# Four taps in place of three ahead of the vector engine, from the second image on, with new order tables

## The reference, cut to what matters

```python
x = x + conv_block(_ln_c(x))          # per image
#   qkv = conv 1x1 (256 -> 768)
#   agg = conv 1x1 grouped(conv 5x5 depthwise(qkv, padding=2))
#   q, k, v of qkv and of agg; relu on q and k
#   out = q (k^T [v, 1]) ; out[..., :-1] / (out[..., -1:] + 1e-15)
#   proj 1x1 (512 -> 256), batch norm with given mean and variance
t = t + ffn(_ln_t(t))                 # 1024 tokens of 256 per image
#   weights of 6 experts from softmax(mean token @ router), top 2 of 11
#   sum over experts of w_e * (gelu(t W1_e + b1_e) W2_e + b2_e)
```

## Time and profile before

| | us |
|---|---|
| median of 3 runs (1488.21 to 1489.84) | 1489.03 |
| the profiled execution, its own time | 1490.25 |
| its span in the trace | 1488.5 |
| PE busy | 1368.5 (92%) |
| DVE busy | 1255.1 (84%) |
| ACT busy | 1058.4 (71%) |
| POOL busy | 964.1 (65%) |

### The profile page before, as it was taken

How to read it: one execution, slowest core, us unless ns; L and a number is a source line. 1 busy time by engine, 2 the same in 40 slices (tenths; PEclk the granted TensorE clock), 3 DMA queues, 4 the chain that set the end, 5 groups by cost and what they waited for, 6 DMA issues and landing times.

```text
span 1488.5 us, 18705 instructions
## 1 busy us (share of the span) xinstructions
PE 1368.5 (92%) x6844; PEld 779.7 (52%) x6844; DVE 1255.1 (84%) x1281; ACT 1058.4 (71%) x1887; POOL 964.1 (65%) x736
## 2 busy tenths in 40 slices
PE   5996788899999999999999999999999998999997
PEld 3445645555655556555655556555655555544343
DVE  5999499999999999999999999999999996950100
ACT  4454465778678877878687877977787857765775
POOL 5265557567678668756776677856865757445644
PEclk8997799899999999999999999999999999999999
DMA  6010000000002000100001000100000000100000
GB/s 227 31 57 0 0 29 1 0 30 15 0 1 72 15 0 1 43 29 15 1 0 72 15 1 1 43 15 0 1 35 9 15 1 1 43 15 1 15 15 15
DMA packets 14251, 32.75 MB, mean 22 GB/s; under 512 B 2384, under 2 KB 5328, under 8 KB 13904
## 3 DMA queue, kind: packets, MB, share of 16 engines
q1 hardware_dynamic: 14160, 31.56, 6.1%
...
## 4 chain that ended last, share of the span: by engine, by line
PE 63%; DVE 16%; ACT 9%; POOL 6%; issue 5%; DMA 1%; SPq 0%; POOLq 0%; ACTq 0%; DVEq 0%
PE wbk L504 23%; PE acc L517 16%; DVE dacc L1125 13%; PE wbk L621 7%; PE wbk L631 3%; PE wbk L595 3%; PE wbk L580 3%; PE wbk L607 3%; PE wbk L575 2%; POOL gl L968 2%; PE wbk L614 1%; ACT hb L735 1%; ACT hb L832 1%; ACT gh L734 1%; POOL dwo L938 1%
## 5 line engine op out<-in xcount | busy, mean ns | idle before, releaser
L1125 DVE SCALAR_TENSOR_TENSOR dacc<-qkvs,dww,dacc 128x960 f32<-128x960 f32 (+4 forms) x930 | 1026.9, 1189 | 0.0
L968 POOL TENSOR_TENSOR gl<-hb,gh 128x512 f16<-128x512 f32 x256 | 303.8, 1194 | 241.3 <-ACT hb L735 239.8
L938 POOL TENSOR_TENSOR dwo<-dwo,tapb 128x992 f32<-128x992 f32 (+2 forms) x100 | 227.2, 2272 | 118.6 <-ACT tapb L709 88.7
L832 ACT ACTIVATE hb<-wbk,b1s 128x512 f32<-128x512 f32 x256 | 174.5, 684 | 113.5 <-PE wbk L504 105.6
L517 PE MATMUL acc<-gh,w2h 128*128 128x512 f16 x512 | 194.9, 381 | 7.1 <-POOL gl L968 6.2
L517 PE MATMUL acc<-gl,w2h 128*128 128x512 f16 x512 | 194.8, 380 | 0.0
L517 PE MATMUL acc<-gh,w2l 128*128 128x512 f16 x512 | 194.7, 380 | 0.0
L734 ACT ACTIVATE gh<-hb,ewg 128x512 f16<-128x512 f32 x256 | 183.3, 716 | 2.6 <-PE acc L517 1.3
L735 ACT ACTIVATE hb<-hb,ewg 128x512 f32<-128x512 f32 x256 | 182.6, 713 | 0.0
L504 PE MATMUL wbk<-th,w1h 128*128 128x512 f16 x512 | 154.1, 383 | 11.7 <-ACT rb L823 4.6
L504 PE MATMUL wbk<-tl,w1h 128*128 128x512 f16 x512 | 153.7, 382 | 0.0
...
## 6 DMA issues: line engine op xcount, KB each, us to landing
...
```

Of the source, the lines that this page charges most:

```text
L832: last = nc.scalar.activation(hb[:, f % GB, :], b[:], ACT.Gelu, bias=b1s[:, f % FT:f % FT + 1], scale=1.0 / (X_SCALE * W_SCALE))
L938: ins = nc.gpsimd.tensor_tensor(d3[:, oy, ox], d3[:, oy, ox], t3[:, iy, ix], ALU.add)
L968: nc.gpsimd.tensor_tensor(gl[:, f % GB, :], hb[:, f % GB, :], gh[:, f % GB, :], ALU.subtract).then_inc(g_low, 1)
L1125: ins = nc.vector.scalar_tensor_tensor(out=dst[:, oy, ox], in0=i3[:, jy, jx], scalar=dww[:, m, tap:tap + 1], in1=a3[:, oy, ox], op0=ALU.mu ...
```

## The change

Image 1's tiles 2 and 3 (the keys of the second image) have no base taps. All other tiles of images 1 to 7 have four in place of three; the fourth is the tap two rows above the centre. Image 0 is as before. All five tables are written anew, and so are the places of DVE's small tasks.

```diff
     if s == 0:
         return DIAG_BASE if m in DIAG_TILES else []
-    return BASE_TAPS[:3]
+    if s == 1 and m in (2, 3):
+        return []
+    return BASE_TAPS[:4]
```

One line of FIRST and one of END, and the places:

```diff
-squares.0.0.0 squares.0.0.1 sums.0.0 weights.0 weights.2 stats.0.0 rnorm.0.0 means.0 rbc.0.0.0 rbc.0.0.1
+squares.0.0.0 squares.0.0.1 sums.0.0 weights.2 weights.0 stats.0.0 rnorm.0.0 rbc.0.0.0 rbc.0.0.1 means.0
...
-apply.-1.1.0 apply.-1.1.1 high.-1.1.0 high.-1.1.1 low.-1.1.0 low.-1.1.1 S G G logits.-1 F S F S G F exp.-1 S
+apply.-1.1.1 F G high.-1.1.0 S high.-1.1.1 low.-1.1.0 F G low.-1.1.1 S F S F logits.-1 exp.-1 G F S G F G G
...
-AGG_PLACES = {1: (20, 24, 76, 81), 2: (17, 25, 78, 87), 7: (20, 23, 75, 84), 8: (19, 21, 75, 83)}
-RAW_PLACES = {0: (89, 90), 1: (64, 68), 2: (66, 72), 7: (69, 74)}
+AGG_PLACES = {1: (20, 25, 75, 80), 2: (17, 23, 79, 82), 7: (16, 20, 80, 84), 8: (19, 21, 75, 83)}
+RAW_PLACES = {0: (86, 87), 1: (63, 66), 2: (66, 67), 7: (66, 72)}
```

More of the change, by code:

```diff
@@ new lines @@
+matrices.0.1 qkv.0.1.0 qkv.0.1.1 sums.1.0 stats.1.0 rnorm.1.0 b b diag.0.0.0 rbc.1.0.0 rbc.1.0.1 apply.1.0.0
+apply.1.0.1 b diag.0.0.1 b diag.0.1.0 high.1.0.0 tok.0.0 b low.1.0.0 high.1.0.1 diag.0.1.1 tok.0.1 tok.0.2
+tok.0.3 tok.0.4 b tok.0.5 b b tok.0.6 tok.0.7 b relu_q.0.0 b kv.0.0.0 b kv.0.0.1 mask.0.0 relu_q.0.1
+att.0.0.0 att.0.0.1 att.0.0.2 att.0.0.3 scale.0.0.0 att.0.0.4 att.0.0.5 att.0.0.6 att.0.0.7 b b scale.0.0.1
+back.0.0.0.0 back.0.0.0.1 back.0.0.1.0 back.0.0.1.1 agg.0.2.0 low.1.0.1 agg.0.2.1 agg.0.3.0 agg.0.3.1
@@ L179 @@
[L179 to L188, removed]
@@ new lines @@
+b b stats.-1.1 kv.0.0.1 mask.0.0 rnorm.-1.1 b F S relu_q.0.1 att.0.0.0 b S att.0.0.1 att.0.0.2 att.0.0.3
+rbc.-1.1.0 rbc.-1.1.1 G F scale.0.0.0 att.0.0.4 apply.-1.1.0 apply.-1.1.1 att.0.0.5 att.0.0.6 att.0.0.7
+scale.0.0.1 qkv.1.2.1 S S G F high.-1.1.0 high.-1.1.1 low.-1.1.0 low.-1.1.1 logits.-1 qkv.1.3.0 back.0.0.0.0
+back.0.0.0.1 back.0.0.1.0 back.0.0.1.1 qkv.1.3.1 G S agg.0.2.0 agg.0.2.1 F exp.-1 squares.2.0.0 F F F
+squares.2.0.1 sums.2.0 agg.0.3.0 agg.0.3.1 G G G S stats.2.0 G G S rnorm.2.0 F F F S b G S G S b G S
@@ L201 @@
[L201 to L205 removed]
+agg.-1.0.0 S F agg.-1.0.1 agg.-1.1.0 agg.-1.1.1 S G att.-1.1.0 att.-1.1.1 att.-1.1.2 G F qkv.0.0.0 G
@@ new lines @@
+rbc.-1.1.0 rbc.-1.1.1 apply.-1.1.0 G F apply.-1.1.1 scale.0.0.0 att.0.0.4 att.0.0.5 att.0.0.6 G S att.0.0.7
+scale.0.0.1 high.-1.1.0 qkv.1.2.0 qkv.1.2.1 high.-1.1.1 F qkv.1.3.0 b S back.0.0.0.0 low.-1.1.0 low.-1.1.1
+logits.-1 b S qkv.1.3.1 back.0.0.0.1 back.0.0.1.0 back.0.0.1.1 agg.0.2.0 G F agg.0.2.1 agg.0.3.0
+squares.2.0.0 squares.2.0.1 sums.2.0 F exp.-1 agg.0.3.1 S b G G stats.2.0 b F F S G G S rnorm.2.0 F G S F F
+G S b S b F S G F agg.0.4.0 rbc.2.0.0 G rbc.2.0.1 apply.2.0.0 S G F agg.0.4.1 S b apply.2.0.1 agg.0.5.0
@@ L218 @@
-G F F agg.0.4.1 S b b agg.0.5.0 agg.0.5.1 G S S G G S F F G S kv.0.1.0 G F F S G F G S G S F b S G kv.0.1.1
-F F S b G G F mask.0.1 S F b b S b G S
+rnorm.-1.1 G G relu_q.0.1 F att.0.0.0 rbc.-1.1.0 rbc.-1.1.1 apply.-1.1.0 apply.-1.1.1 att.0.0.1 att.0.0.2 F
+b att.0.0.3 scale.0.0.0 att.0.0.4 att.0.0.5 G att.0.0.6 att.0.0.7 S b high.-1.1.0 F high.-1.1.1 low.-1.1.0 S
+scale.0.0.1 low.-1.1.1 S G F logits.-1 back.0.0.0.0 back.0.0.0.1 back.0.0.1.0 back.0.0.1.1 F S G exp.-1 G G
+S F agg.0.2.0 agg.0.2.1 agg.0.3.0 agg.0.3.1 F G F b S G b G F b S b F S G F S S G S F agg.0.4.0 G F F G S F
```

74 lines of the change are left out of this document (33 added, 41 removed).

## The result

The changed kernel takes 1497.86 us (median of 4 runs, 1496.82 to 1498.33) against 1488.72 (1488.21 to 1489.84): the ratio is 1.0059, 95% interval 1.0042 to 1.0077. It is 9 us slower where 9 us faster was forecast, outside the range of 1470 to 1492. The same kernel beside later experiments took 1496.06, ratio 1.0047 (1.0033 to 1.0061).

A forecast was written before the change was run, and what follows sets the result against it. PE, busy 1368.5 of 1488.5 us, was taken to set the end. Gains of 3 (ramp), 2.5 (middle), 1.5 (stage 7) and 2.5 (stage 8) sum to 9.5, giving 1480 us; own range 1473 to 1487, wider range 1470 to 1492.

The forecast's parts named there:

- Set-up: Start of the run: means go behind the norm's factors, so DVE's taps of image 0 start about 3.4 us later.
- Stage 7: Image 7's stage: an F and an attention product fill PE's 3.07 us wait between rnorm and rbc; 1.5 us gained.
- Ramp: Start of image 1: POOL's sums come earlier, PE reaches image 0's second attention near 197, not 201.35; 3 us gained.
- Middle: Stages 2 to 6: base taps moved to where ACT waits; 0.5 us off each of five images, 2.5 us.
- The two waits named: PE's middle waits of 0.87 us for rb and 1.70 us, with base tap moved or routing's exp and F reordered.
- relief of DVE in the middle is thus worth little by itself: Middle images: PE sets the end, its waits there are for ACT's evictions, none for DVE.
- Stage 8: Last stage: F, S, F, S, F, S fill PE's 3.71 us wait before the last F and logits; 2.5 us gained.
- Slower, by ACT: Rival: between an F and its S, half of 36 new taps hold back evictions PE needs; 1503 us, chance 0.12.
- The exclusion bites: Rival: in stage 7 four L1117 each wait 1.7 us more beside POOL, PE waits for DVE; 1485 us, chance 0.05.
- The vector engine governs: Rival: PE's ramp hangs on DVE's start of image 1, 19 us of waits go in full; 1466 us, chance 0.08.

The follow-up runs named there:

- e2: Changed kernel with weights.0 ahead of weights.2 again in FIRST, means left behind the rbc words: 1493.07 us, ratio 1.0025.
- e3: Changed kernel with the first ten words of FIRST as in the kernel before (weights.0 ahead of weights.2, means ahead of rbc): 1490.24 us, ratio 1.0007.
- e5_both: Changed kernel with the first ten words of FIRST as in the kernel before and three b words added to LAST: 1484.73 us, ratio 0.9970.
- e7_no_key_taps: Kernel before with no base taps for image 1's keys (tiles 2 and 3), three elsewhere, all tables as before: 1487.58 us, ratio 0.9992.

## Why the prediction was wrong, point by point

- **Set-up: the step that failed is one the sum didn't have.** The swap of `weights.2` and `weights.0`, in the same line of the diff, got no price. It cost 3.6 to 4.2 at the start of the taps. The text took the factors at PE "at about 23.3" from a trace in which w_qkv was copied before w2 (the earlier trace rows don't show that figure; POOL's power ends at 23.07 there). The means were priced at 3.4 us and cost 3.4, but by luck: DVE took them 6.1 us later (33.99 in e2 against 27.86 in e3), not 4.3, and 2.8 of it went in the instructions behind, where the text had 0.9.
- **Stage 7: the sum had +1.5 for one stall and didn't count the taps.** The 3.07 us at `rbc` did go. But the prediction counted 136 base adds in all and never set the 18 words `b` of LAST against the 11 taps that they had to serve before the last pair. That is a count of words in a table, needs no trace, and would have shown the 9th to 11th behind the attention. Cost 9.85, of which 6.4 went with three added words; the other 3.4 are open, but for the clock that goes with most of them.
- **Ramp: the way to the attention was right, what came behind it wasn't.** L642 began at 178.3 (not 173) and the attention at 202.3 (not 197); most of that is the unpriced copy, since with both set-up lines restored they stand at 170.7 and 194.7. The attention is then 6.6 us ahead of the kernel before, and at stage 2 only 1.6 to 2.9 are left (348.57 less 345.67 or 344.35, the marks of e5_both and e3_setup_order, less 1.3 for the S). The sum's 3 us stood after 3.4 lost in the set-up, so it asked for 6.4. The 2.3 us that it took off for image 0's second norm were too few: in the changed kernel PE waits 5.87 us at 266.1 for ACT's split before the logits and 3.37 at 283.4 for a gelu, where its longest wait around that norm was 2.93 before. That is read from the traces; no run took SECOND apart. The end of image 0's taps, put at 171, was at 176.1.
- **Middle: the size a little low, the reason not borne out.** 3.4 us in all in place of 2.5, 0.84 per full period in place of 0.5. The two waits named did go, and PE's longest wait for POOL there is 0.6. But "relief of DVE in the middle is thus worth little by itself" doesn't hold for the new tables: with three taps the period is 1.8 us longer, and 1.05 of that, by the trace, comes by way of DVE's reciprocal. The rows that were read, PE's releasers, can't show an engine that acts through another one's queue.
- **Stage 8:** right in kind, 3.9 in place of 2.5, the upper bound 3.7.
- **The rivals.** "Slower, by ACT" (0.12, 1503) is nearest: in stage 7 the new taps did stand before evictions that PE needed, on ACT and on POOL. But it was three taps, by their place, and not half of 36. "The exclusion bites" named stage 7 as the place; it bit in the set-up, in another pair of instructions. "The vector engine governs" is half right: in e7_no_key_taps it governs stage 2.
